# Edge attention of a graph network: fewer signals from TensorE, fewer waits for them

## The reference

```python
def _conv_per_edge(x_src, edge_attr, edge_sh, Wang, Wlin, W1, b1, W2):
    rad = relu(edge_attr @ W1 + b1) @ W2          # radial layers
    g = edge_sh @ Wang.T                          # gates
    return x_src * g @ Wlin * rad
q = (node_attr @ Wq).reshape(n, H, DQ // H)
k = _conv_per_edge(node_attr[src], edge_attr, edge_sh, Wang_k, Wlin_k, W1k, b1k, W2k)   # E x 64
v = _conv_per_edge(node_attr[src], edge_attr, edge_sh, Wang_v, Wlin_v, W1v, b1v, W2v)   # E x 128
alpha = einsum("ehq,qk,ehk->eh", q[dst], Wdot, k)
ealpha = exp(alpha - segment_max(alpha, dst)[dst])
out = segment_sum((ealpha / segment_sum(ealpha, dst)[dst]) * v, dst) @ Wout
```

## Time and profile before

| | us |
|---|---|
| time of the runs, median of 3 | 4299.97 (4298.48 to 4300.72) |
| span of the profiled execution | 5039.6 |
| TensorE busy in it, matmuls | 4108.6 (82%) |
| VectorE busy | 3024.4 (60%) |
| ScalarE busy | 1972.1 (39%) |
| GpSimd busy | 1919.0 (38%) |

### The profile page before, as it was taken

One profiled execution on the slowest core, in us unless ns is written; L12 is line 12 of the kernel. 1 busy time (PEld: TensorE's weight loads), 2 busy tenths in 40 slices (PEclk: granted clock), 3 DMA queues, 4 the chain that ended last, 5 costly groups with the idle time before them and its releaser, 6 DMA issues. The chain is left out here.

```text
span 5039.6 us, 74127 instructions
## 1 busy us (share of the span) xinstructions
PE 4108.6 (82%) x26543; PEld 3350.2 (66%) x26543; DVE 3024.4 (60%) x4129; ACT 1972.1 (39%) x2885; POOL 1919.0 (38%) x2002
## 2 busy tenths in 40 slices
PE   4667999999999984688888888888888888888832
PEld 4656999999999973465665666666666566666622
DVE  8985544544444342566666666666666666666734
ACT  5754666655665531222222223222223222222313
POOL 5640000000000015555555555555555555555352
PEclk9878999999999985799989999999999999999965
DMA  7998999999998533455555665556666655566433
GB/s 169 188 188 263 298 295 297 294 295 297 292 292 267 182 101 94 133 163 163 164 156 152 166 163 161 162 165 166 164 163 164 166 164 157 159 164 164 141 114 47
DMA packets 1012838, 944.08 MB, mean 187 GB/s; under 512 B 705677, under 2 KB 811929, under 8 KB 1012339
## 3 DMA queue, kind: packets, MB, share of 16 engines
q1 hardware_dynamic: 952099, 814.71, 55.7%
q0 software_dynamic: 60368, 124.52, 11.1%
HBM read 648.66 MB, written 289.97 MB: 186 GB/s over the span
## 5 line engine op out<-in xcount | busy, mean ns | idle before, releaser
L2313 POOL DMA_INDIRECT feats_hops<-x_table,src_s x1616 | 1546.9, 957 | 1223.1 <-PE e_turn_ps L2423 771.8
L1286 PE MATMUL acc<-t_wide,scaled 128*128 128x448 f32 x6860 | 1409.0, 366 | 24.2 <-DVE t_wide L1380 24.2
L1286 PEld LDWEIGHTS acc<-t_wide,scaled 128*128 128x128 f32 x6860 | 1284.3, 188 | 129.2 <-DVE scaled L1398 24.6
L1321 ACT CAST t_wide<-t_ring 128x1568 fp32r<-128x1568 uint8 x490 | 737.7, 1506 | 564.9 <-PE acc L1286 543.8
L1380 DVE CAST t_wide<-t_ring 128x1568 fp32r<-128x1568 uint8 x490 | 478.3, 976 | 733.4 <-PE acc L1286 714.9
L2484 ACT COPY e_out_rows<-e_turn_ps 128x512 f32<-128x512 f32 x404 | 222.1, 588 | 1026.5 <-remote 932.5
L1809 POOL MEMSET l_eps<- 128x1 f32 x1 | 0.1, 104 | 1452.9 <-POOLq L1498 1452.9
L2423 PE MATMUL e_turn_ps<-ident,feats_hops 128*128 128x128 f32 x1616 | 250.3, 296 | 355.6 <-ACT e_out_rows L2484 292.4
L2401 PE MATMUL e_ring_ps<-e_wlin_v,e_x_gv 128*128 128x128 f32 x3232 | 432.7, 281 | 96.9 <-issue 85.6
L2401 PEld LDWEIGHTS e_ring_ps<-e_wlin_v,e_x_gv 128*128 128x128 f32 x3232 | 393.0, 194 | 115.9 <-issue 102.2
L2569 DVE TENSOR_TENSOR e_lw<-e_ring_ps,e_w_t 128x1024 f32<-128x1024 f32 x202 | 247.1, 1223 | 366.9 <-remote 249.6
(11 more groups left out here) (272 smaller groups left out, 5096.2 us busy)
## 6 DMA issues: line engine op xcount, KB each, us to landing
t_ring<-adjacency_bytes SPq DMA_DIRECT2D x490, 512.0 KB, 5.8
sums_table<-e_out_rows SPq DMA_DIRECT2D x202, 576.0 KB
q_first<-hop_zeros_q SPq DMA_DIRECT2D x101, 512.0 KB, 5.9
e_sh<-parts_sh SPq DMA_DIRECT2D x404, 128.0 KB
e_ea<-parts_ea SPq DMA_DIRECT2D x404, 128.0 KB
e_q_rows<-q_first SPq DMA_DIRECT2D x404, 128.0 KB
e_same<-same_row SPq DMA_DIRECT2D x404, 128.0 KB
adjacency_bytes<-lists_staged SPq DMA_DIRECT2D x196, 256.0 KB
```

The source lines that it names most:

```text
L1286: mm = nc.tensor.matmul(acc[c][:, 0:n], U[p][:, b, :], wide[m % WIDE_RING][:, lo:lo + n], start=(b == 0 and p == 0), stop=(b == NB - 1 and ...
L1321: nc.scalar.copy(into, of).then_inc(wide_act, 1)
L2313: nc.gpsimd.indirect_dma_start(x_rows[i % XR][:, g * GT + t, :], None, x1_table, bass.IndirectOffsetOnAxis(ap=src_ix[:, at:at + 1], axis=0 ...
```

## The change

TensorE raises one semaphore where it raised two: `p_keys` behind the keys stands for `p_rk` and `p_lk`, `p_hid`, `p_xt` and `p_seg` rise once behind the second half, and `p_gates` behind the value gates stands for `p_gv` and `p_q`. For that the transposes of the queries move ahead of both gates. `p_score` rises only behind the last step of a batch (and the last two steps of all). Waits that another signal of TensorE now implies are left out.

```diff
+        def told(i):
+            return i % BATCH == BATCH - 1 or i >= N - 2
+
+        def scores_told(i):
+            return sum(told(m) for m in range(i + 1))
...
                 if i >= 2:
-                    sp.wait_ge(p_gv, i - 1)
+                    sp.wait_ge(p_gates, i - 1)
...
                 if i >= 2:
-                    sp.wait_ge(p_hid, 2 * (i - 1))
+                    sp.wait_ge(p_hid, i - 1)
...
-                if i >= 2:
-                    sp.wait_ge(p_q, i - 1)
...
                 if i >= XR:
-                    pool.wait_ge(p_xt, 2 * (i - XR + 1))
+                    pool.wait_ge(p_xt, i - XR + 1)
...
             def spread_out(j, i):
...
-                    mm.then_inc(p_seg, 1)
+                mm.then_inc(p_seg, 1)
...
             def scores(i):
...
-                mm.then_inc(p_score, 1)
+                if told(i):
+                    mm.then_inc(p_score, 1)
...
             def keys_and_radial(i):
...
-                nc.tensor.matmul(bank[:, 1, :], w2k[:], hid_k[s][:], start=True, stop=True).then_inc(p_rk, 1)
+                nc.tensor.matmul(bank[:, 1, :], w2k[:], hid_k[s][:], start=True, stop=True)
...
-                mm.then_inc(p_lk, 1)
+                mm.then_inc(p_keys, 1)
...
             def turn_x(r, i):
...
-                    tr.then_inc(p_xt, 1)
+                tr.then_inc(p_xt, 1)
...
             def hidden(r, i):
...
-                    nc.tensor.matmul(turn_ps[:, n, :], stack[:, n * D:(n + 1) * D], ea[s][:],
-                                     start=True, stop=True).then_inc(p_hid, 1)
+                    mm = nc.tensor.matmul(turn_ps[:, n, :], stack[:, n * D:(n + 1) * D], ea[s][:], start=True, stop=True)
+                mm.then_inc(p_hid, 1)
...
             def turn_q(r):
...
-                tr.then_inc(p_q, 1)
...
                     hidden(i + 1, i)
+                    turn_q(i + 1)
                     gates(i + 1, 0, p_gk)
-                    gates(i + 1, 1, p_gv)
-                    turn_q(i + 1)
+                    gates(i + 1, 1, p_gates)
...
             def keep_rows(j):
...
+                act.wait_ge(p_seg, j + 1)
                 for h in range(2):
-                    act.wait_ge(p_seg, 2 * j + h + 1)
...
             def keep_x(r):
...
+                act.wait_ge(p_xt, r + 1)
                 for h in range(2):
-                    act.wait_ge(p_xt, 2 * r + h + 1)
...
             def keep_hidden(r):
-                act.wait_ge(p_hid, 2 * r + 1)
+                act.wait_ge(p_hid, r + 1)
                 if r >= 2:
-                    act.wait_ge(p_rk, r - 1)
+                    act.wait_ge(p_keys, r - 1)
...
-                act.wait_ge(p_hid, 2 * r + 2)
...
             def gate(i):
...
-                if i >= 2:
-                    dve.wait_ge(p_lk, i - 1)
...
-                dve.wait_ge(p_gv, i + 1)
+                dve.wait_ge(p_gates, i + 1)
...
             def find_spots(i, j):
-                dve.wait_ge(p_score, min(i - 1, N))
+                if i >= N:
+                    dve.wait_ge(p_score, scores_told(min(i - 2, N - 1)))
...
             def spread_queries(i):
...
-                dve.wait_ge(p_q, i + 1)
...
             def keys(i):
...
-                dve.wait_ge(p_rk, i + 1)
+                dve.wait_ge(p_keys, i + 1)
...
-                dve.wait_ge(p_lk, i + 1)
                 dve.wait_ge(v_rkq, i + 1)
-                if i >= 2:
-                    dve.wait_ge(p_score, i - 1)
...
             def find_most(n):
...
-                dve.wait_ge(p_score, scored_by(n))
+                dve.wait_ge(p_score, scores_told(min((n + 1) * BATCH, N) - 1))
```

More of the change, by code:

```diff
@@ L2221, in edge_attention @@
         stored = sems("stored")
-        p_xt, p_gk, p_gv, p_hid, p_q = sem("p_xt"), sem("p_gk"), sem("p_gv"), sem("p_hid"), sem("p_q")
-        p_lk, p_rk, p_score = sem("p_lk"), sem("p_rk"), sem("p_score")
+        p_xt, p_gk, p_gates, p_hid = sem("p_xt"), sem("p_gk"), sem("p_gates"), sem("p_hid")
+        p_keys, p_score = sem("p_keys"), sem("p_score")
         p_lv, p_rv, p_seg, p_wt = sem("p_lv"), sem("p_rv"), sem("p_seg"), sem("p_wt")
@@ L2240, in chain_at @@
             return n if p == 0 and 0 <= n < NBATCH else None
-        def scored_by(n):
-            return min((n + 1) * BATCH, N)
+        def told(i):
+            return i % BATCH == BATCH - 1 or i >= N - 2
+        def scores_told(i):
+            return sum(told(m) for m in range(i + 1))
         ITERATIONS = range(-1, N + LAG + 1)
@@ L2442, in turn_q @@
                 for t in range(GT):
-                    tr = nc.tensor.transpose(q_ps[:, t * P:(t + 1) * P], q_rows[s][:, t, :, :].rearrange("p g q -> p (g q)"), ident[:])
-                tr.then_inc(p_q, 1)
+                    nc.tensor.transpose(q_ps[:, t * P:(t + 1) * P], q_rows[s][:, t, :, :].rearrange("p g q -> p (g q)"), ident[:])
             def gates(r, n, done):
@@ L2553, in find_spots @@
             def find_spots(i, j):
-                dve.wait_ge(p_score, min(i - 1, N))
+                if i >= N:
+                    dve.wait_ge(p_score, scores_told(min(i - 2, N - 1)))
                 nc.vector.tensor_copy(score_ps[:, 2 * P:2 * P + K], fpos[:, j * K:(j + 1) * K]).then_inc(v_spot, 1)
                 if j >= 2:
-                    dve.wait_ge(p_seg, 2 * (j - 1))
+                    dve.wait_ge(p_seg, j - 1)
                 dve.wait_ge(v_spot, 2 * j + 1)
```

## The result

The changed kernel takes 4323.24 us (median of 4, 4317.11 to 4324.12), the kernel before 4300.21 us beside it: ratio 1.0052, 95% interval 1.0041 to 1.0064. It is slower by 23 us; 4316 was predicted.

The account below looks back on a forecast made before the run. TensorE was taken to bound the kernel, busy in propagation and nearly so in undisturbed attention steps of 10.06 us. Terms of 0.45 + 0.18 - 0.30 = 0.33 us per batch, times 50, gave 4316 us from 4300; range 4245 to 4340.

Parts of the forecast that it names:

- The base: Edge attention: runs taken to spend near 10.06 us a step, not the profile's 13.82; change costed on 4300 us.
- the rival of late signals: Attention steps: late signals remain in the runs and fewer are less late; faster, 4276 us (4237 to 4316), chance 0.31.
- Another pace: Attention steps: something else, the transfers, paces the step and hides the 0.33 us per batch; same, 4300 us, chance 0.30.
- Signals free for TensorE: Every attention step: 5.75 fewer TensorE signals gain 0; by the skill's 26.3 ns each, 31 us at most.
- The scan step: Step with the batch scans: the product chain comes 0.58 us later against 0.13 margin, so TensorE waits 0.45 us.
- the sum: Per batch 0.45 + 0.18 - 0.30 = 0.33 us, over 50 batches 16.5 us: 4316 us.
- The step behind: Step after the batch scans: the second gate's wait for `prod`, 0.30 us per batch before, goes: 0.30 us back.
- The batch transposes: Once per batch, `turn_weights` waits for both copies of turned rows: 0.18 us per batch, bounds 0 and 0.44.
- the loss: Per batch, 0.45 us at the scan step's values and 0.18 us at the batch transposes.
- the credit: Second gate in the step behind the scans: 0.30 us back per batch; alone, -15 us (4285).
- The plain step: Attention step without batch scans or transposes: later signals are covered, so it costs nothing.
- the brittle pipeline: Copies starting together make TensorE wait 0.44 us more each step, 89 us: 4389 us, chance 0.03.

Follow-up runs that it names:

- the queries first: Kernel before with one edit, the transposes of the queries moved ahead of both gates, all signals as before: 4278.39 us (ratio 0.9951).
- both apart: Changed kernel with separate signals again for keys and radial keys, and for each half of the turned rows: 4279.41 us (ratio 0.9953 to the kernel before).

## Why the prediction was right

- *The base.* The steps without late signals were the ones to cost in, though only plain and scan steps take the 10.06 us; the four of a batch average 10.34. The unchanged kernel's second profile has plain steps of 10.05 us and a DMA share of 0.80 in the stretch 2400 to 4000 us, the share that was worked out for a step of 10.3. That the lateness goes with the gathers was wrong: 4296.9 us with the same gathers and none of it. With it falls the rival of late signals; fewer signals gained nothing. Another pace falls too: at the same DMA share of 0.80 TensorE is busy 1599.83 of 1600 us with the queries first.
- *Signals free for TensorE.* Held, as far as the runs go: 14 signals with the queries first and 10.25 with both apart differ by 1 us. The serialized increments of the Trainium skill ("TensorE: Matmul & The Clock Gate", "The cost: per-tile semaphore tail") would make 20 us of these 3.75 signals and 31 us of all 5.75, as an estimate, if every one lay on the path. No run here shows such a gain; why it stays away was not tested.
- *The scan step.* `rkq` starts 6.03 us behind the values (3031.16 less 3025.13), where it stood at 5.44 in the kernel before (3019.33 less 3013.89): 0.59 us later, 0.58 foretold. The first weight load of the next values stands at 10.40 us in place of 9.95: the 0.45 of the sum. The step itself grows by 0.35 us, 10.41 for 10.06; the other 0.10 falls into the step behind, whose first load runs 0.01 us ahead of its matmul in place of 0.11 and whose values take 2.05 us in place of 1.95.
- *The step behind.* 10.28 instead of 10.59: 0.31 us back for the 0.30 of the sum, and this match is luck. The step was 0.54 us over a plain one before, not 0.30, and it keeps 0.21 where the sum left nothing: 0.10 from the scan step, 0.11 at the second gate. `prod` comes late by about what was foretold (7.67 us behind the values, the gate's place at 7.38), but the step loses more than the wait for it. Its weight load, which has to wait too, starts only 0.12 us behind `prod` and 0.03 us ahead of its matmul (3031.74, 3031.77); whether that is all of the rest was not tested.
- *The batch transposes.* 11.05 instead of 10.67: 0.38 us for the 0.18 of the sum. This is the term that was too small, and it stood between its bounds of 0 and 0.44. The copies end as foretold, at 3.98 us behind the values; the first weight load follows them by 0.23 us (3007.99 to 3008.22), and its matmul stands 0.40 us later than in the kernel before (4.24 for 3.84).
- *The sum.* 0.35 - 0.31 + 0.38 = 0.42 us per batch, 21 us over 50 batches, for 0.33 and 16.5. Sorted by cause it is 0.45 for the scans, 0.38 for the transposes and 0.43 back at the second gate (0.54 less 0.11): the loss was put 0.20 too low and the credit 0.13 too low, and the two misses partly cancel. The plain step is unchanged (10.07 for 10.05), and the brittle pipeline did not come: copies that start together cost nothing in it.

## What to carry to other kernels

Where one engine is busy without a gap, a signal merged onto the last of several instructions delays whoever could have begun behind the first, and it is paid for where the busy engine in turn waits for that one; look for it first in the few steps where a consumer's slack is already used up (here those of the batch scans and transposes). With the slack gone the plain step pays too: 0.30 us of it with the keys merged and the queries left behind the gates. The gain in such a change can sit in its side effect: moving four transposes ahead of the gates, which only served to share a signal, gave a waiting instruction some 0.4 us of cover and alone makes the kernel 0.5% faster. And when a profile's span is 17% above the timed runs, first ask which of its stretches can be that much shorter, and cost the change in the step that fits the runs.

## What the runs showed of the hardware that was not expected

In one profiled execution of the kernel before, TensorE's signals reached their waiters microseconds late (4.5 us in the earlier trace rows), and its steps took 13.82 us on average. It was not ScalarE alone, whose copy of the sums also waits for an earlier store: in the same step VectorE's `lw`, which waits for no transfer, starts 2.65 us behind the end of its values (3213.82).

```profile
3216.47 1.23 DVE L2569 TENSOR_TENSOR e_lw<-e_ring_ps,e_w_t 128x1024 f32<-128x1024 f32 x1 [3.32 <-remote]
```

The profile models the ends of matmuls, so it can't tell a late signal from a matmul that ended later than shown. In the eight other profiles, of the same code, of the changed kernel and of six variants with 9.25 to 14 signals a step, no such step stands between 2400 and 4000 us (the longest takes 11.3 us), and the timed runs have no room for it. What disturbed that execution is open: no run here repeated it.
